# Results of the last routed pages summed by TensorE with 0/1 matrices instead of scattered: a mixture-of-experts layer on one core

## What is computed

```python
def _L1_ffn_ref(hidden_states, gate_w, e_bias, up_w, down_w, shared_up_w, shared_down_w):
    ...
    topk_idx, topk_w = _router(x, gate_w, e_bias)      # 6 of 32 experts per token
    combine = jnp.zeros((T, N_EXPERTS), topk_w.dtype).at[jnp.arange(T)[:, None], topk_idx].add(topk_w)
    h = _relu2(jnp.einsum('th,eih->tei', x, up_w))
    h = h * combine[:, :, None]
    moe_out = jnp.einsum('tei,ehi->th', h, down_w)
    shared = _relu2(x @ shared_up_w.T) @ shared_down_w.T
    return (moe_out + shared).reshape(B, S, H)
```

## Time and profile before

| | us |
|---|---|
| median of 3 runs | 887.16 |
| lowest and highest | 883.94, 887.17 |
| the profiled execution, its own time | 888.47 |
| its span, from the first to the last instruction | 886.6 |
| mean granted TensorE clock, share of full | 0.903 |

### The profile page before, as it was taken

How to read it: one execution, slowest core, us unless ns; L and a number is a source line. 1 busy time by engine, 2 the same in 40 slices (tenths; PEclk the granted TensorE clock), 3 DMA queues, 4 the chain that set the end, 5 groups by cost and what they waited for, 6 DMA issues and landing times.

```text
span 886.6 us, 14153 instructions
## 1 busy us (share of the span) xinstructions
PE 722.6 (82%) x4526; PEld 631.4 (71%) x4526; DVE 416.7 (47%) x1615; ACT 273.0 (31%) x620; POOL 308.5 (35%) x322
## 2 busy tenths in 40 slices
PE   3868886389999999999899888866776868787865
PEld 2647776289999999999899877533456757676754
DVE  4998664022333243546644742725104444456563
ACT  2636631022111111222223122321123455445540
POOL 1333307600010111100552354172712656556560
PEclk9898859589999999999999998796978899989998
DMA  8999992231776767755866624242646556587866
GB/s 257 396 296 268 257 252 97 102 125 53 231 231 219 218 221 244 246 169 190 304 218 232 217 89 170 92 166 87 217 154 189 177 158 191 164 288 243 285 215 250
DMA packets 93534, 181.22 MB, mean 204 GB/s; under 512 B 9857, under 2 KB 54998, under 8 KB 93182
## 3 DMA queue, kind: packets, MB, share of 16 engines
q1 hardware_dynamic: 78048, 138.67, 50.9%
q0 software_dynamic: 13344, 38.68, 11.6%
q10 hardware_dynamic: 2046, 2.71, 1.0%
HBM read 134.07 MB, written 65.62 MB: 225 GB/s over the span
## 4 chain that ended last, share of the span: by engine, by line
PE 56%; DVE 16%; issue 10%; another core or an unknown queue 6%; DMA 4%; ACT 3%; POOL 3%; SPq 1%; DVEq 0%; POOLq 0%; ACTq 0%
PE PB L618 16%; PE PB L655 11%; PE PB L632 5%; PE PB L825 4%; PE PB L816 4%; PE PB L763 3%; POOL rows_out L1930 3%; PE PB L777 2%; PE PB L804 2%; DMA X<-in_x 2%; PE PB L684 1%; PE PB L600 1%; DMA MEM<-rows_out 1%; DVE WK L1256 1%
## 5 line engine op out<-in xcount | busy, mean ns | idle before, releaser
L618 PE MATMUL PB<-XT,MEM 128*128 128x128 f32 x1584 | 185.9, 276 | 1.1 <-issue 1.1
L618 PEld LDWEIGHTS PB<-XT,MEM 128*128 128x128 f32 x1584 | 181.7, 193 | 1.5 <-issue 1.3
L1882 POOL DMA_INDIRECT sorted_y<-WK x36 | 34.5, 958 | 279.0 <-DVE WK L1470 279.0
L1891 POOL DMA_INDIRECT rows_in<-MEM x96 | 93.5, 974 | 65.1 <-DVE MEM L1674 36.6
L655 PE MATMUL PB<-MEM,WK 128*128 x432 | 99.7, 380 | 3.3 <-DVE MEM L1646 1.9
L825 PE MATMUL PB<-MEM,WK 128*128 x228 | 67.6, 424 | 32.0 <-DVE WK L1823 26.1
L655 PEld LDWEIGHTS PB<-MEM,WK 128*128 128x128 f32 x432 | 79.3, 190 | 13.2 <-issue 3.9
L1930 POOL DMA_INDIRECT rows_out<-WS,MEM x58 | 56.7, 977 | 64.4 <-ACT WS L1045 49.2
L825 PEld LDWEIGHTS PB<-MEM,WK 128*128 128x128 f32 x228 | 42.2, 207 | 41.2 <-issue 36.9
L1930 POOL DMA_INDIRECT rows_out<-MEM x56 | 56.2, 1003 | 40.5 <-ACT MEM L1045 25.7
L939 ACT ACTIVATE XT<-PB 128x256 f32<-128x256 f32 x52 | 19.8, 381 | 162.2 <-PE PB L600 134.2
(11 more groups left out here) (280 smaller groups left out, 1255.4 us busy)
## 6 DMA issues: line engine op xcount, KB each, us to landing
MEM<-in_w SPq DMA_DIRECT2D x36, 896.0 KB
rows_in<-in_consts SPq DMA_DIRECT2D x32, 600.0 KB, 12.2
MEM<-in_w SPq DMA_DIRECT2D x36, 512.0 KB
MEM<-rows_in SPq DMA_DIRECT2D x58, 300.0 KB
MEM<-rows_out SPq DMA_DIRECT2D x16, 768.0 KB, 7.0
MEM<-in_w SPq DMA_DIRECT2D x32, 256.0 KB, 2.8
MEM<-in_w SPq DMA_DIRECT2D x2, 3072.0 KB, 18.9
sorted_x<-MEM SPq DMA_DIRECT2D x1, 5070.0 KB, 39.7
```

The source lines that it names most:

```text
L618: t = e.matmul(o[:, to:to + P], UPW[m][i % (3 - m)][:, k, c * P:(c + 1) * P], XT[:, n % 2, k, :], start=(k == 0), stop=(k == 1))
L1882: e.indirect_dma_start(out=DY, out_offset=bass.IndirectOffsetOnAxis(ap=DEST[:, i:i + 1], axis=0), in_=YS[:, i % 2, :], in_offset=None).the ...
L1891: e.indirect_dma_start(out=DX1, out_offset=bass.IndirectOffsetOnAxis(ap=SLOT1[:, i, j:j + 1], axis=0), in_=XR[:, i, :], in_offset=None).th ...
```

## The change

Pages from 104 on (`OWN` is 52, the first such pair) hold rows of group 3 alone. Their results are no longer scattered. For such a page ScalarE writes the weighted results to one of four buffers YO. VectorE writes a 128 x 512 matrix HOT that is 1 where a row of the page belongs to one of the 512 tokens of group 3 (`one_hot`, from a constant TOKENS that SP loads in step 30). TensorE multiplies for each of the four tiles HOT's 128 x 128 part by the 128 x 256 results and accumulates in PSUM banks 6 and 7 (`to_tokens`). At the end VectorE adds these banks to X. The up product then uses two banks and not four. The rows of group 3 in `rows_out` are cleared beforehand, by four DMAs of SP during the first layer's blocks, since not all are written.

All eight loads of tiles 8 to 15 then wait only for the scatters of pages up to 103, and stand in SP's program behind the store of tiles 6 and 7. Tiles 8, 10, 12 and 14 are added up by GpSimd, with the four instructions of `sum_rows`. VectorE's sums of tiles 6 and 7 move from steps 54 and 56 to steps 53 and 54.

```diff
+OWN = (TOPK * GB[3] + E1) // 2
+def up_bank(s):
+    return 4 + s % (4 if s < OWN - 2 else 2)
...
+            def to_tokens(s, n_pairs):
+                q.wait_ge("by", s)
+                q.wait_ge("hot", s)
+                q.wait_ge("bh", OWN - 3)
+                for b in (2 * s, 2 * s + 1):
+                    last = b == 2 * n_pairs - 1
+                    for i in range(4):
+                        t = e.matmul(PB[:, 6 + i // 2, i % 2 * D:(i % 2 + 1) * D], HOT[b % 4][:, i * P:(i + 1) * P], YO[b % 4],
+                                     start=(b == 2 * OWN and i % 2 == 0), stop=last, skip_group_check=True)
+                        if last and i == 1:
+                            t.then_inc(*q.mark("owned", 0))
+                t.then_inc(*(q.mark("owned", 1) if last else q.mark("own", s)))
...
+                if OWN <= s - 2 < n_pairs:
+                    to_tokens(s - 2, n_pairs)
...
-                for i in range(8, NT, 2):
-                    o = PB[:, i // 2, 0:D]
...
-                    for k in range(TOPK):
-                        e.matmul(o, ident, Y6[place(i)][:, k * D:(k + 1) * D], start=(k == 0), stop=False)
...
+                            if r >= OWN + 2:
+                                q.wait_ge("own", r - 2)
+                            to = YO[b % 4]
...
+            def one_hot(s):
+                q.wait_ge("in_tokens")
...
+                for b in (2 * s, 2 * s + 1):
+                    t = e.tensor_scalar(HOT[b % 4], TOKENS, PT6[:, s // 2 % 2, b % 4:b % 4 + 1], None, ALU.is_equal)
+                t.then_inc(*q.mark("hot", s))
...
+                if OWN <= s - 1 < n_pairs:
+                    one_hot(s - 1)
...
-                if s in (54, 56):
-                    whole(sum_rows(s // 2 - 21))
+                if s in (53, 54):
+                    whole(sum_rows(s - 47))
...
                 for i in range(9, NT, 2):
                     whole(sum_rows(i))
+                    if i > GB[3]:
+                        h = (i - GB[3]) // 2
+                        q.wait_ge("sv", i)
+                        q.wait_ge("sp", i - 1)
+                        q.wait_ge("owned", h)
+                        e.tensor_tensor(X[:, i - 1:i + 1, :], X[:, i - 1:i + 1, :],
+                                        PB[:, 6 + h, :].rearrange("p (t d) -> p t d", t=2), ALU.add).then_inc(
+                            *q.mark("total", h))
...
-            for s in range(-1, COMMON):
+            q.wait_ge("zeroed1", 12)
+            for s in range(-1, OWN + 2):
                 step(s, 58)
...
+            for i in range(8, NT, 2):
+                y = Y6[place(i)]
+                q.wait_ge(f"l6_{place(i)}", i)
+                e.tensor_tensor(y[:, 0:3 * D], y[:, 0:3 * D], y[:, 3 * D:6 * D], ALU.add).then_inc(*q.mark("set1"))
...
+                if i in (6, 8, 10, 12):
+                    lo = TRASH + (GB[3] + i // 2 - 3) * P * TOPK
+                    e.dma_start(DY1[lo:lo + P * TOPK, :].rearrange("(p n) d -> p n d", p=P),
...
+            store(6)
+            for i in range(8, NT):
+                fetch6(i)
```

More of the change, by code:

```diff
@@ L60, in shape_constants @@
 def shape_constants():
-    c = np.zeros((P, NC_ + RW), np.float32)
+    c = np.zeros((P, NC_ + RW + 4 * P), np.float32)
+    c[:, NC_ + RW:] = (GB[3] * P + np.arange(4 * P)) * TOPK + TRASH
     c[:, CI:CI + P] = np.eye(P, dtype=np.float32)
@@ L1065, in end1 @@
                     step(s, n_pairs)
-                for i in range(8, NT, 2):
-                    q.wait_ge("sum", i)
-                    e.activation(X[:, i, :], PB[:, i // 2, 0:D], ACT.Copy).then_inc(*q.mark("end", i))
-                    q.wait_ge("end", i)
-                    q.wait_ge("sv", i + 1)
+                for h in range(2):
+                    i = GB[3] + 2 * h
+                    q.wait_ge("total", h)
                     e.dma_start(od[:, i:i + 2, :], X[:, i:i + 2, :]).then_inc(*q.land("out_b", i))
@@ L1932, in step @@
                             in_=YB[b // 8 % 2][:, b % 8, :], in_offset=None).then_inc(*q.land(f"yb{b % 16}", b))
-            for s in range(-1, COMMON):
+            q.wait_ge("zeroed1", 12)
+            for s in range(-1, OWN + 2):
                 step(s, 58)
-            def end1(c):
-                n_pairs = PAIRS[c]
-                for s in range(COMMON, n_pairs + 2):
-                    step(s, n_pairs)
-            q.copies(number1, [2 * n for n in PAIRS], end1)
+            for i in range(8, NT, 2):
+                y = Y6[place(i)]
+                q.wait_ge(f"l6_{place(i)}", i)
+                e.tensor_tensor(y[:, 0:3 * D], y[:, 0:3 * D], y[:, 3 * D:6 * D], ALU.add).then_inc(*q.mark("set1"))
+                for k in (1, 2):
+                    q.wait_ge(*q.last)
+                    e.tensor_tensor(y[:, 0:D], y[:, 0:D], y[:, k * D:(k + 1) * D], ALU.add).then_inc(*q.mark("set1"))
+                q.wait_ge(*q.last)
+                q.wait_ge("drn", GROUP[i])
+                e.tensor_tensor(X[:, i, :], X[:, i, :], y[:, 0:D], ALU.add).then_inc(*q.mark("sp", i))
         def sp_program(q):
@@ L2093, in step @@
                 if s in FETCH6:
-                    fetch6(FETCH6[s], n_pairs)
+                    fetch6(FETCH6[s])
                 if s - 3 in SUM6 and SUM6[s - 3] % 2:
                     store(SUM6[s - 3] - 1)
-                if s == 56:
-                    store(6)
+                if s == 30:
+                    q.wait_ge("d1", len(UNITS) - 1)
+                    e.dma_start(TOKENS, consts[:, NC_ + RW:NC_ + RW + 4 * P]).then_inc(*q.land("in_tokens"))
                 return fetched
```

65 lines of the change are left out of this document (34 added, 31 removed).

## The result

The changed kernel takes 897.19 us (median of 20 runs, 891.71 to 902.41), the kernel before 887.93 on the same chip (20 runs, 878.86 to 898.59): 1.0119 times as long, 95% interval 1.0095 to 1.0143. It is slower, and its time lies outside the predicted 882.5 to 893.5 us. The profiled execution took 894.78 us with a span of 892.9, against 888.47 and 886.6.

What follows compares the result with a forecast made beforehand. Two chains behind the page loop bound it: TensorE's new products (886.5 us) and eight loads plus sums (887.5). The later, 0.9 over the 886.6 span, added to the 887.16 median gave 888.1 us; 8-in-10 range 882.5 to 893.5.

Steps and rivals of the forecast that it cites:

- 877.1 without and 880.5 with a pause: End of TensorE's new products behind the page loop, 880.5 us including one ScalarE pause of 3.4 us.
- the first rival: At the last two pairs, a pause halves TensorE's clock and 32 records cost twice: median 894.0 us; chance 0.19.
- the third: In the first layer, the clearing DMAs aren't hidden and hold its blocks, 8 us: median 896.1 us; chance 0.05.
- the 880.1 that I wrote: Landing of tile 15, last of eight loads behind one another, one every 2.3 us from 864.0 us.
- my lower bound of 877.3: Landing of tile 15 if the eight loads go at the best rate shown, 1.9 us each.
- chain 2: Group 3's eight loads, then VectorE's last sum and addition, shared time with GpSimd, store and end: 887.5 us.
- it keeps up: GpSimd's sums of even tiles at the end: 3.6 us a tile against one landing every 4.6 us.
- I add the 1.3 us in full: After tile 15 lands, GpSimd and VectorE exclude each other for 1.3 us; lower bound zero.
- the 881.4 that I wrote: End of GpSimd's sum of tile 14, which lands at 877.8 us and takes 3.6 us.
- 3.1 us from VectorE's last operation: Store and end behind VectorE's last operation, 3.1 us as in the kernel before.
- which was in no one's way: GpSimd loses its branch; listed under what costs nothing, so no time was counted.
- 887.5: Predicted span in us, set by the loads and the sums behind them, against 886.6 before.

Runs made afterwards that it cites:

- e1: Kernel before plus only the four clearing DMAs in the first layer's blocks and GpSimd's wait for them; ratio to the kernel before 1.0013, repeat 1.0009.
- e2: Changed kernel with GpSimd's sums of tiles 8, 10, 12 and 14 replaced by one-column memsets (result incomplete); ratio to the kernel before 0.9963.
- a1: Changed kernel unaltered, run again on a chip whose page loop has no pauses; ratio to the kernel before 1.0078.
- e6: Changed kernel, but TensorE adds tiles 12 and 14, VectorE the other six; loads ahead of the store, last down product earlier; ratio to before 0.9965, repeat 0.9964.
- e8: Kernel before plus one GpSimd memset of a 128x1 column after VectorE's sum of tile 15; ratio to the kernel before 1.0000.

## Why the prediction was wrong

What held, by the profile of the changed kernel. The first load of tile 8 goes out at 860.09 (I wrote 859). Pair 52's results come at 852.59, 1.2 later than before. Sixteen records of a pair's new products take 3.46 to 3.73 us on the chain (3.44), and the last ends at 879.13 between the 877.1 without and 880.5 with a pause. TensorE's clock stays at 1.00 up to 880, so the first rival did not happen. That the time it gave, 894.0, and that of the third, 896.1, lie near the measured 897.19 is luck; e1 and the table's first column rule the third out. The loads went at about their best rate: the DMA share falls to 0.44 from 876 on, so tile 15 was in well before the 880.1 that I wrote, nearer my lower bound of 877.3. This term was too long, which worked against the errors below.

**The step that failed is the end of chain 2**, "it keeps up", said of GpSimd, and "I add the 1.3 us in full". The shared time of the two engines was counted for the last 1.3 us only, and the end behind it taken over from before. Three terms of it:

- GpSimd's tile. I took 3.6 us, with 1.42 for the 768 columns by the slope of two shorter operations in the earlier trace rows. Alone the 768 columns take it 1.80 and the tile 4.17, beside VectorE's sums 5.07. Tiles 10 and 12 land 4.6 us apart as I wrote (868.34 and 872.90), but that is too fast for it. Four tiles at 4.17 behind 864.56 would have ended at 881.2, so the wrong size alone would have done no harm to the 881.4 that I wrote. Beside VectorE they end at 884.11.
- The exclusion. I had the right rule and counted it for the last 1.3 us only, as if the engines worked in turns until then. GpSimd adds without a gap from 864.56 on, beside VectorE's matrices from 865.14 and its sums from 871.05. VectorE's row from 868.22 to 888.54 holds 0.9 + 4 x 2.3 + 2 x 0.7 = 11.5 us of its own work; the other 8.8 are the stretching of its operations. The last addition ends at 888.54 instead of 884.4, 4.1 us. In e2, without GpSimd's sums, the end comes 7.9 us sooner on its chip.
- The end. I carried over 3.1 us from VectorE's last operation. It was 4.4, since GpSimd's drain ends later than the last store; on the chip of a1 it was 6.9. I had written that GpSimd loses its branch, "which was in no one's way", and put nothing down for it. The long drain stands in every program without the branch; that the branch is its cause isn't shown.

4.1 + 1.3 is 5.4 us, and 887.5 + 5.4 is the measured span of 892.9. The last two terms aren't independent, since the later of two rows sets the end. Estimates from the numbers above: without the drain the span would have been 891.4 (890.91 + 0.46); with the drain and no stretching of GpSimd it could not have been under 890.1 (881.24 + 8.84).

Behind these stands who sums the even tiles now. Before, TensorE did so with L856 while it waited for loads. The prediction took these products off TensorE as work that had cost nothing, and let GpSimd do it for nothing too; in fact it was paid for in VectorE's time. e6 gives half of it back to TensorE, the other half to VectorE, and with its new order turns the loss into a gain of 0.35%.

What stays open: the medians on the first chip differ by 9.3 us, and the traces place 4.2. The same kernel has 1.0119 there, 1.0025 on a second chip and 1.0078 on a third, with intervals that exclude each other in part. All that the traces say is that nothing ahead of pair 52's results differs by more than one execution does from the next. What the pauses are isn't known either.

## What to carry to other kernels

Before work goes to an idle engine, price it beside what the other engines do in the same microseconds, over the whole overlap and for both sides: for GpSimd beside VectorE the pair of tiles took 5.07 us, not 4.17. If both then show 95% busy, compare with one of them doing it all. Work that an engine did while it waited anyway (TensorE's sums) is best left there when the rest is moved. And look at which engine finishes last in the program, not only which is busy last: a queue that used to be empty long before the end may bring its own drain into it.

## What the runs showed of the hardware

- VectorE and GpSimd, both with two SBUF inputs: 768 columns 0.95 and 1.80 us alone, 1.48 and 1.98 together; 256 columns 0.42 and 0.72 alone, 0.83 and 0.79 to 1.32 together, at times 1.91 on VectorE. One tile on each, side by side: 5.07 us, against 6.42 one after the other. The matrices (a tensor_scalar over 512 columns, one SBUF input) went from 0.48 to 1.51 us as well. The Trainium skill (SBUF — State Buffer, section Who interferes with whom) names tensor_scalar among the VectorE operations that can enter a two-port mode and then contend with GpSimd; the 1.51 us beside 0.48 agree with that, and I had left it out.
- GpSimd's closing drain ended 8.6 us behind its last operation in each trace of the changed program, whatever that operation was, and 1.75 us behind it in e8. What decides it isn't known.
- One program takes 775 us on some chips and 888 to 898 on others, with the pauses of the earlier trace rows present only on the latter. The changed kernel has 1.0078 on one of the first kind, 1.0119 and 1.0025 on two of the second, so the kind alone doesn't order the ratios.
